# State scan of a 2D selective-scan block: GpSimd in pairs of states, another split of the products, earlier loads

## The reference

```python
E, R, N = 192, 6, 16
...
xs = jnp.stack([xf, xf[..., ::-1], xt, xt[..., ::-1]], axis=1)
dbc = jnp.einsum('bkcl,krc->bkrl', xs, x_proj_w)
dlt, b, c = (dbc[:, :, :R], dbc[:, :, R:R + N], dbc[:, :, R + N:])
...
phi = jnp.exp(-jnp.cumsum(dA, axis=3))
dbx = dlt[..., None] * jnp.swapaxes(b, 2, 3)[:, :, None] * xs[..., None]
h = phi * jnp.cumsum(dbx / (phi + 1e-12), axis=3)
y = jnp.einsum('bkdln,bknl->bkdl', h, c) + Ds[None, :, :, None]
```

## Time and profile before

| What | us |
|---|---|
| median of 3 runs (2992.67 to 2995.89) | 2993.05 |
| the profiled execution, its own time | 2992.62 |
| its span, first to last instruction | 2990.7 |
| state scan: first `b_r` to last product with C | 301.80 to 2017.13 |
| VectorE busy over the whole span | 2566.7 (86%) |
| GpSimd busy over the whole span | 1986.8 (66%) |
| TensorE matmuls busy over the whole span | 2196.5 (73%) |
| ScalarE busy over the whole span | 1572.6 (53%) |

### The profile page before, as it was taken

The page is one execution under the profiler, slowest core; times in us unless marked ns, Lnnn a source line. Parts: engine busy times, 40 slices in busy tenths (PEclk is TensorE's granted clock), DMA queues, the critical chain, the costliest instruction groups (busy, mean ns, idle before and its releaser), DMA issues. The chain is left out here.

```text
span 2990.7 us, 25217 instructions
## 1 busy us (share of the span) xinstructions
PE 2196.5 (73%) x7484; PEld 1085.7 (36%) x7484; DVE 2566.7 (86%) x2150; ACT 1572.6 (53%) x2301; POOL 1986.8 (66%) x1119
## 2 busy tenths in 40 slices
PE   6843667677776767777766677777985999798579
PEld 3421223333333333333323333334442555354444
DVE  5667999999999999999999999996787777699620
ACT  2565767677677766777777677763230000362220
POOL 0164999999999999999999999994000000297000
PEclk9977899999999999999999999998997999899689
DMA  1286333333443433333343433325005443100360
GB/s 47 87 236 236 101 107 115 105 120 99 119 113 114 121 101 120 103 119 109 116 120 105 119 105 114 120 79 188 0 0 140 116 126 95 37 8 16 78 87 24
DMA packets 144679, 304.05 MB, mean 102 GB/s; under 512 B 53596, under 2 KB 69217, under 8 KB 139553
## 3 DMA queue, kind: packets, MB, share of 16 engines
q1 hardware_dynamic: 143456, 298.31, 34.5%
q10 hardware_dynamic: 1088, 4.13, 0.6%
HBM read 215.59 MB, written 46.87 MB: 88 GB/s over the span
## 5 line engine op out<-in xcount | busy, mean ns | idle before, releaser
L834 POOL TENSOR_TENSOR l0c_r<-l0c_r,l0c_v 128x768 f32<-128x768 f32 x576 | 1038.9, 1816 | 27.0 <-DVE l0c_r L797 26.2
L864 ACT ACTIVATE ps<-l0c_dlt,l0c_na 128x512 f32<-128x512 f32 (+1 forms) x1152 | 626.0, 575 | 518.1 <-DVE l0c_h L823 503.9
L843 POOL TENSOR_TENSOR l0c_hcp<-l0c_cb,l0c_h 128x768 f32<-128x768 f32 x384 | 697.9, 1818 | 1.5 <-DVE l0c_h L823 1.5
L823 DVE TENSOR_TENSOR_SCAN l0c_h<-ps,l0c_h,l0c_r 128x768 f32<-128x768 f32 x384 | 692.8, 1804 | 1.2 <-issue 1.2
L755 PE MATMUL ps<-l0c_hcp,net_ident 128*128 128x512 f32 (+1 forms) x1536 | 591.5, 509 | 15.1 <-ACT l_Z L857 7.3
L874 ACT ACTIVATE l0c_r<-l0c_S,l0c_floor,l0c_na 128x768 f32<-128x768 f32 x576 | 579.7, 1013 | 0.0
L722 PE MATMUL ps<-l0c_Bp,l0c_sel 96*128 96x512 bf16 (+1 forms) x1152 | 297.4, 341 | 384.0 <-DVE l0c_hcv L804 224.6
L797 DVE SCALAR_TENSOR_TENSOR l0c_r<-l0c_r,ps 128x768 f32<-128x768 f32 x576 | 533.3, 926 | 13.8 <-PE ps L722 7.8
L755 PEld LDWEIGHTS ps<-l0c_hcp,net_ident 128*128 128x128 f32 x1536 | 273.0, 198 | 267.1 <-issue 202.9
L823 DVE TENSOR_TENSOR_SCAN l0c_h<-ps,l0c_r 128x768 f32<-128x768 f32 x192 | 335.1, 1745 | 1.0
L1526 PE MATMUL ps<-l_prod,l_wa 128*96 128x384 f32 (+1 forms) x888 | 292.3, 493 | 25.6 <-DVE l_prod L1443 25.6
(11 more groups left out here) (273 smaller groups left out, 2290.6 us busy)
## 6 DMA issues: line engine op xcount, KB each, us to landing
l0c_cb<-cf SPq DMA_DIRECT2D x768, 192.0 KB, 3.4
l_other<-l_p SPq DMA_DIRECT2D x22, 864.0 KB, 5.9
dlt<-l0s_dl SPq DMA_DIRECT2D x36, 384.0 KB, 2.3
v<-l0s_vv SPq DMA_DIRECT2D x36, 384.0 KB, 2.9
l0c_dlt<-dlt SPq DMA_DIRECT2D x36, 384.0 KB, 3.9
l0c_v<-v SPq DMA_DIRECT2D x36, 384.0 KB, 4.4
l_other<-l_p SPq DMA_DIRECT2D x22, 288.0 KB, 6.7
l0c_Bp<-bc SPq DMA_DIRECT2D x36, 144.0 KB, 4.0
```

The lines of the kernel that those rows point to most:

```text
L823: dve.tensor_tensor_scan(h[:, n, :], da[j % 2], r[:, j % NR, :], init, ALU.mult, ALU.add).then_inc(s_scan, 1)
L834: pool.tensor_tensor(r[:, j % NR, :], r[:, j % NR, :], v[:, (j // N) % 2, :], ALU.mult).then_inc(s_w, 1)
L843: pool.tensor_tensor(hcp[:, p % NHP, :], cb[:, p % NCB, :], h[:, e % N, :], ALU.mult).then_inc(s_hp, 1)
L864: act.activation(da[e % 2][:, part], dlt[:, i, part], ACT.Exp, scale=na[:, i, n:n + 1]).then_inc(done, 1)
```

## The change

- `by_pool` becomes a table. Of 16 states VectorE takes the products with C of 2, 5, 10, 13 in even units (called A in what follows) and of 2, 5, 8, 11, 12, 15 in odd units (B). The rest falls into neighbouring pairs, 6 in an A unit and 5 in a B unit.
- GpSimd works on two states with one instruction: the product with v on j and j + 1, where `v` is read twice, and the product with C on one of those pairs. Each waits for both of its states (`s_ub` of j + 1, `s_scan` of e + 1).
- One DMA now brings the C rows of two states to 64 partitions; the ring is as large as before, two pairs.
- `r` has 8 tiles instead of 6, `hcv` 3 instead of 2; `b_r` runs 4 ahead instead of 3, `tanh` 6 ahead of the decay instead of 5, `add_y` 5 behind instead of 3, and the store moves from n = 8 to n = 11.
- `loads(u + 1)` stands behind n = 2 in SP's order and waits for the first scan of unit u instead of a store.
- The very last product with C (state 575) is VectorE's now.

```diff
-        NR, NHV, NHP, NCB = 6, 2, 4, 4
-        AHEAD = 3
+        NR, NHV, NHP, NCB = 8, 3, 4, 4
+        AHEAD, LATE, LAG = 4, 5, 6
+        BY_VECTOR = ((2, 5, 10, 13), (2, 5, 8, 11, 12, 15))
...
-        s_cb = [sem(f"cb{i}") for i in range(NCB)]
+        s_cb = [sem(f"cb{i}") for i in range(NCB // 2)]
...
+        with_c = [u * N + n for u in range(U) for n in BY_VECTOR[u % len(BY_VECTOR)]]
+        others = [j for j in range(J) if j not in with_c]
+        taken = [sum(i < j for i in with_c) for j in range(J + 1)]
+        assert all(b == a + 1 and a // N == b // N for a, b in zip(others[::2], others[1::2]))
...
-            return j % 3 != 0
+            return j not in with_c
...
-            return (j + 2) // 3
+            return taken[j]
...
-            return j - dve_steps(j)
+            return j - taken[j]
...
                 if u >= 2:
-                    sp.wait_ge(s_evac, u - 1)
+                    sp.wait_ge(s_scan, (u - 1) * N + 1)
...
             for j in range(J):
...
-                if by_pool(j):
+                if by_pool(j) and pool_steps(j) % 2 == 0:
...
                     p = pool_steps(j)
...
-                        sp.wait_ge(s_hp, p - NCB + 1)
+                        sp.wait_ge(s_hp, p - NCB + 2)
                     for i in range(2):
-                        sp.dma_start(cb[64 * i:64 * i + 64, p % NCB, :],
-                                     d["cf"][k, 2 * t + i, n:n + 1, c0:c0 + SEG].to_broadcast([64, SEG])
-                                     ).then_inc(s_cb[p % NCB], 16)
-                if n == (0 if u == 0 else 8) and u + 1 < U:
+                        sp.dma_start(cb[64 * i:64 * i + 64, p % NCB:p % NCB + 2, :],
+                                     d["cf"][k, 2 * t + i, n:n + 2, c0:c0 + SEG].unsqueeze(0)
+                                     .to_broadcast([64, 2, SEG])).then_inc(s_cb[p % NCB // 2], 16)
+                if n == (0 if u == 0 else 2) and u + 1 < U:
...
             for i in range(2):
...
-                    pe.wait_ge(s_hp, pool_steps(j) + 1)
+                    pe.wait_ge(s_hp, pool_steps(j) // 2 * 2 + 2)
...
-            for j in range(J + 3):
+            for j in range(J + LATE):
                 if j < J and not by_pool(j):
                     c_rows(j)
...
-                if j >= 3:
-                    add_y(j - 3)
+                if j >= LATE:
+                    add_y(j - LATE)
...
             def times_c(j):
...
-                if j >= 3 * NHV:
-                    dve.wait_ge(s_y, j - 3 * NHV + 1)
+                if dve_steps(j) >= NHV:
+                    dve.wait_ge(s_y, with_c[dve_steps(j) - NHV] + 1)
...
-            assert by_pool(J - 1)
+            if not by_pool(J - 1):
+                times_c(J - 1)
...
-            for j in range(J + AHEAD + 1):
+            def times_v(j):
+                if j % N == 0:
+                    pool.wait_ge(s_in[(j // N) % 2], (j // N // 2 + 1) * (16 * NLOAD))
+                pool.wait_ge(s_ub, j + 2)
+                two = r[:, j % NR:j % NR + 2, :]
+                pool.tensor_tensor(two, two, v[:, (j // N) % 2, :].unsqueeze(1).to_broadcast([128, 2, SEG]), ALU.mult
+                                   ).then_inc(s_w, 2)
+            def times_c(e):
+                p = pool_steps(e)
+                pool.wait_ge(s_scan, e + 2)
+                pool.wait_ge(s_cb[p % NCB // 2], 32 * (p // NCB + 1))
+                if p >= NHP:
+                    pool.wait_ge(s_y, others[p - NHP + 1] + 1)
+                pool.tensor_tensor(hcp[:, p % NHP:p % NHP + 2, :], cb[:, p % NCB:p % NCB + 2, :],
+                                   h[:, e % N:e % N + 2, :], ALU.mult).then_inc(s_hp, 2)
+            for j in range(0, J + AHEAD + 2, 2):
                 if j < J:
-                    if j % N == 0:
-                        pool.wait_ge(s_in[(j // N) % 2], (j // N // 2 + 1) * (16 * NLOAD))
-                    pool.wait_ge(s_ub, j + 1)
-                    pool.tensor_tensor(r[:, j % NR, :], r[:, j % NR, :], v[:, (j // N) % 2, :], ALU.mult
-                                       ).then_inc(s_w, 1)
-                e = j - AHEAD - 1
-                if e >= 0 and by_pool(e):
-                    p = pool_steps(e)
-                    pool.wait_ge(s_scan, e + 1)
-                    pool.wait_ge(s_cb[p % NCB], 32 * (p // NCB + 1))
-                    if e >= 6:
-                        pool.wait_ge(s_y, e - 5)
-                    pool.tensor_tensor(hcp[:, p % NHP, :], cb[:, p % NCB, :], h[:, e % N, :], ALU.mult
-                                       ).then_inc(s_hp, 1)
+                    times_v(j)
+                for e in (j - 5, j - 4):
+                    if 0 <= e and e + 1 < J and by_pool(e) and pool_steps(e) % 2 == 0:
+                        times_c(e)
...
-            LAG = NR - 1
+            FIRST, LAST = LAG + LATE, N - 1
...
-                if n == LAG + 3 and 0 < u < U:
+                if n == FIRST and 0 < u < U:
...
-                late = 0 < u < U and LAG + 3 <= n < LAG + 8
+                late = 0 < u < U and FIRST <= n < LAST
...
-                    if 0 < u and n == LAG + 8:
+                    if 0 < u and n == LAST:
...
-                elif late and n > LAG + 3:
+                elif late and n > FIRST:
```

More of the change, by code:

```diff
@@ L712, in _ @@
                 sp.wait_ge(s_sel[i], 16 * ((T + 1 - i) // 2))
-            for i in range(NCB):
-                sp.wait_ge(s_cb[i], 32 * pool_steps(J) // NCB)
+            for i in range(NCB // 2):
+                sp.wait_ge(s_cb[i], 32 * len(range(2 * i, pool_steps(J), NCB)))
         @block.tensor
```

## The result

| | us |
|---|---|
| before, median of 4 runs (2990.62 to 2995.89) | 2992.86 |
| changed kernel, median of 4 runs (2972.95 to 2974.61) | 2973.65 |
| ratio, 95% interval | 0.9933 (0.9919 to 0.9948) |
| profiled execution of the changed kernel: its own time, its span | 2974.61, 2972.7 |

The changed kernel takes 19 us less, which is more than the 0.2% that can be told from no change. The forecast of 2980 had the direction, and a size of 12.5 where 19 came; 2973.65 lies 0.35 us under the range of 2974 to 2991.

The account below looks back on a forecast made before the run. The prediction took VectorE to bound the kernel, with GpSimd close behind. Its terms, -11.3 + 1.1 + 1.8 - 4.1 = -12.5 us against the profiled 2992.6, gave 2980 us, range 2974 to 2991 for 8 in 10.

Parts of the forecast that it names:

- What bounds: State scan: VectorE sets the pace, 46.9 us a unit after the change; GpSimd follows with 45.9 at 3.40 a pair.
- Term 1: VectorE's products with C fall from 192 to 180, the last one after the last scan: -11.3 us.
- Term 2: Start of the stage: five `b_r` before the first scan instead of four, one saved later: +1.1 us.
- Term 4: VectorE's waits for B rows, mostly after the cumsum: half of 8.2 us goes, -4.1; ends 0 and -8.2.
- Term 3: End of the stage: three TensorE additions follow GpSimd's last pair, +1.8 us; at the lower clock 4 us more.
- Term 5: Larger rings, C rows of two states per DMA and the moved loads: costed at nothing.
- The rival in which GpSimd ends last: State scan: GpSimd becomes the bound from 3.47 us a pair on; at 3.54, 3003 us; chance 13%.
- TensorE late: TensorE's additions wait for whole pairs and delay VectorE's B rows: about 2991 us, half of that 2986; chance 10%.

Follow-up runs that it names:

- single instructions: Changed kernel, but GpSimd works each pair of states as two instructions of one state: 3013.51 us, ratio 1.006.
- four products everywhere: Changed kernel, but VectorE takes the products with C of 2, 5, 10, 13 in every unit: 3000.7 us, ratio 1.0025.
- all shifted: Changed kernel with 168 products for VectorE, three tables in turn, each with n = 0 instead of 2: 2986.62 us, ratio 0.9976.

## Why the prediction was wrong in size, point by point

The stage became 19.9 us shorter in the profiled executions (1716.95 to 1697.03), the sum of my terms was 12.5.

| term | forecast | measured |
|---|---|---|
| 1. products with C, 13 x 0.87 | -11.3 | -11.3 |
| 2. start, first `b_r` to first scan 6.70, now 8.64; less one later `b_r` | +1.1 | +1.1 |
| 3. end, 5.9 us behind the scan of state 574, now 8.45 | +1.8 | +2.5 |
| 4. waits for B rows | -4.1 (0 to -8.2) | -12.3 |
| sum | -12.5 | -20.0 |

- **What bounds**: right. VectorE stays the bound at 99%, GpSimd falls to 97.5%, and its pairs take the 3.40 us that the line through 480, 768 and 1152 elements gave.
- **Term 1** is right: 180 products at 0.867.
- **Term 2** is right.
- **Term 4 is the step that failed**, twice in its size and once in its reason. I read the size of the waits from the list, 8.2 us, and took it as their upper end; the distances between starts show 12.3. And I took half of it, because k = 0 has no extra matmuls to fill the gap at the cumsum; but before the change k = 0 and k = 1 had only some 1.2 us of delay each over the rest, and k = 2 and 3 some 5 each, so that the units which keep the gap had hardly any delay to keep. The reason that I gave, TensorE idle in the gap and then 0.84 us for its B rows, left out two things. 0.84 us is their time at the lower clock (0.49 at full), and the gap delays VectorE only where extra matmuls stand in front of the B rows as well. Three places make up the term, as the tables above show: n = 12 (-6.6), where the place of the extra matmuls was tested in both directions and every delay stands at the lower clock; n = 5 (-3.6), behind the store of y, tested by moving the product away, again with every delay at the lower clock, and uneven between executions (3.9, 3.3 and 8.0 us in the three traces with the old order there); and n = 9 (-1.8). For n = 9 there was no run, and its cause is argued from rows only. The trace of before shows ScalarE making up two `tanh` there, so that the decay starts only at 617.21 and the scan at 617.75 instead of 616.75 + 0.85 = 617.60; in the changed kernel the making up stands in front of the cumsum.

```profile
615.37 1.93 ACT L874 ACTIVATE l0c_r<-l0c_S,l0c_floor,l0c_na 128x768 f32<-128x768 f32 x2
617.21 1.07 ACT L864 ACTIVATE ps<-l0c_dlt,l0c_na 128x256 f32<-128x256 f32 x2
...
616.75 0.92 DVE L797 SCALAR_TENSOR_TENSOR l0c_r<-l0c_r,ps 128x768 f32<-128x768 f32 x1
617.75 1.76 DVE L823 TENSOR_TENSOR_SCAN l0c_h<-ps,l0c_r 128x768 f32<-128x768 f32 x1
```

- **Term 3** was 0.7 us too small (its own numbers add up to +1.7, not +1.8): I counted three additions behind the last pair, and TensorE had seven behind the pair before. The upper end, a lower clock there, did not come: PEclk is 1.00 from 1989 to 2002.
- **Term 5**, costed at nothing, was right only for the change as a whole. My reason (the loads were on time before) would have held for loads left at n = 8 too, and that costs 95 us. I had asked how long a place in the ring is free, and not what stands behind it in SP's order. The C rows also take longer than I took from the earlier trace rows: two states land in 5.5 us in the changed kernel, where the row of another tile of 384 KB had 4.4.
- **The rival in which GpSimd ends last** did not come, but its threshold was as near as said: single instructions (3.54 for two states) and four products everywhere both cross it. It then costs more than I worked out (3013.5 against 3003), for it shows through TensorE's order as well. **TensorE late** did not come in the changed kernel: its one wait for GpSimd is at the end. In three experiments it did (single instructions, four products everywhere, all shifted).

## What to carry to other kernels

When two engines are full to within a per cent or two, the order decides and not the sums of work: two tables with the same 168 products lay 17 us apart, and adding up release, deadline and work per turn, with the latency of a release in it, put them in the right order, though it missed the path through TensorE's additions. Measure the small delays of the bounding engine by the distances of starts, by place in the loop; a list of waits left out a third of them here. Put the granted clock beside a late TensorE row: all the delays at two places of this loop stood where it was below full, and a price read from such a row (0.84 us) was not the price at full clock (0.49). And when a ring's places come free in larger lumps, look at what stands behind its refill in the queue: loads that had been issued 12 us ahead of their use became 5 us late.

## What the runs showed of the hardware

Elementwise products of two f32 inputs on GpSimd lie on one line from 480 over 768 to 1536 elements in each partition: 1.16, 1.77 and 3.40 us from start to start, 2.12 ns an element and 0.14 us for the instruction. VectorE's scan and `b_r` take the same distances with GpSimd working on pairs as with single states (1.72 and 0.85). When GpSimd waits for a `b_r`, it starts 0.22 to 0.28 us behind the point at which VectorE can start its next instruction (34 waits in the changed kernel; 0.15 to 0.26 in the 26 of the kernel before). A scan that waits for GpSimd's product starts 0.13 us behind the end of that product (62 waits with four products everywhere).

TensorE was granted its lower clock in short stretches: an addition of four matmuls took 1.46 us at 1.00 and 2.93 at the lower level (PEclk 0.53 over that stretch), two matmuls for B rows 0.49 and 0.84. After the same 2.28 us of idling in the same order the clock fell in one execution and stayed in another. The mean granted clock of an execution was 0.924 to 0.933 in all those of the kernel before that were timed beside the experiments, and 0.940 to 0.944 in the four of the changed kernel.
